# Projections by features: both token halves behind each other for every row group and product

## What is computed

```
xn  = layernorm(x)                                  # 625 x 1024
h   = relu(xn @ W_self0 + mean(xn) @ W_neigh0 + b0) # graph, first layer
x  += h @ W_self1 + mean(h) @ W_neigh1 + b1         # second layer
q, k, v = xn @ Wq, xn @ Wk, xn @ Wv                 # 16 heads of 64
q = softmax(q, features) / 8;  k = softmax(k, tokens)
x  += (q @ (k.T @ v)) @ Wo + bo
xn2 = layernorm(x)
gate, up = xn2 @ shared_gate_up                     # 1024 + 1024 columns
shared   = sigmoid(xn2 @ shared_gate_w) * ((silu(gate) * up) @ shared_down)
x  += routed(xn2, top 2 of 8 experts) + shared
```

## Time and profile before

| | before |
|---|---|
| median of 3 runs | 1042.11 us |
| the profiled execution | 1042.34 us |
| its span, first to last instruction | 1040.6 us |
| instructions | 16076 |
| matmuls, weight loads | 6128, 6128 |
| granted TensorE clock | 1.00 |
| HBM | 149 GB/s over the span |

### The profile page before, as it was taken

One profiled execution on the slowest core, in us unless ns is written; L12 is line 12 of the kernel. 1 busy time (PEld: TensorE's weight loads), 2 busy tenths in 40 slices (PEclk: granted clock), 3 DMA queues, 4 the chain that ended last, 5 costly groups with the idle time before them and its releaser, 6 DMA issues.

```text
span 1040.6 us, 16076 instructions
## 1 busy us (share of the span) xinstructions
PE 1024.7 (98%) x6128; PEld 905.3 (87%) x6128; DVE 650.5 (63%) x962; ACT 460.3 (44%) x731; POOL 77.2 (7%) x123
## 2 busy tenths in 40 slices
PE   7999999999999999999999999999999999999998
PEld 5889998787888899987878899998989789998977
DVE  6789968666655765334337364224878588776646
ACT  4423344557777523220122342212666576655530
POOL 6000010000000000000000017000100101000003
PEclk9999999999999999999999999999999999999999
DMA  9821212033212221262200524233789698887618
GB/s 351 314 82 52 71 41 82 11 110 123 81 63 79 82 81 43 106 213 82 81 1 1 181 82 122 89 116 125 265 300 342 223 339 311 278 283 245 227 38 299
DMA packets 76694, 156.44 MB, mean 150 GB/s; under 512 B 8489, under 2 KB 8987, under 8 KB 76618
## 3 DMA queue, kind: packets, MB, share of 16 engines
q1 hardware_dynamic: 65656, 127.30, 35.3%
q0 software_dynamic: 6416, 20.00, 5.5%
q10 hardware_dynamic: 4546, 8.10, 2.1%
HBM read 133.89 MB, written 21.49 MB: 149 GB/s over the span
## 4 chain that ended last, share of the span: by engine, by line
PE 87%; DVE 4%; ACT 3%; DMA 2%; DVEq 2%; issue 1%; POOL 1%; POOLq 0%; ACTq 0%; SPq 0%
PE ps L1988 20%; PE ps L1990 20%; PE ps L1989 20%; PE ps L2452 7%; PE ps L2477 3%; PE ps L2453 3%; PE ps L2087 1%; PE ps L2478 1%; PE ps L2319 1%; PE ps L2250 1%; PE ps L2320 1%; PE ps L2251 1%; PE ps L2101 1%; PE ps L2034 1%; DMA y_second<-expert_rows,slots 1%
## 5 line engine op out<-in xcount | busy, mean ns | idle before, releaser
L1199 DVE TENSOR_TENSOR w_lo<-w_raw,w_hi 128x2048 fp32r<-128x2048 f32 x41 | 93.1, 2289 | 38.6 <-ACT w_hi L801 36.5
L2452 PE MATMUL ps<-xe,w_hi 128*128 128x304 f32 (+2 forms) x384 | 107.1, 356 | 0.0
L1988 PE MATMUL ps<-w_hi,xt_hi 128*128 128x512 f32 (+1 forms) x240 | 95.9, 400 | 3.5 <-DVEq L1509 2.0
L801 ACT CAST w_hi<-w_raw 128x2048 fp32r<-128x2048 f32 x41 | 77.2, 1908 | 45.0 <-PE ps L2320 36.2
L1193 DVE TENSOR_TENSOR w_lo<-w_raw,w_hi 128x1024 fp32r<-128x1024 f32 x68 | 79.8, 1221 | 24.1 <-ACT w_hi L797 22.2
L2453 PE MATMUL ps<-xe,w_lo 128*128 128x152 f32 (+2 forms) x384 | 94.4, 246 | 0.0
L1990 PE MATMUL ps<-w_hi,xt_lo 128*128 128x512 f32 (+1 forms) x240 | 93.7, 390 | 0.0
L1989 PE MATMUL ps<-w_lo,xt_hi 128*128 128x512 f32 (+1 forms) x240 | 93.6, 390 | 0.0
L1193 DVE TENSOR_TENSOR w_lo<-w_late,w_hi 128x1024 fp32r<-128x1024 f32 x64 | 75.2, 1222 | 20.7 <-ACT w_hi L797 18.3
L797 ACT CAST w_hi<-w_late 128x1024 fp32r<-128x1024 f32 x64 | 63.0, 1054 | 38.7 <-PE ps L1990 18.4
L1988 PE MATMUL ps<-xt_hi,w_hi 128*128 128x314 f32 x256 | 79.4, 310 | 0.0
(11 more groups left out here) (371 smaller groups left out, 2365.4 us busy)
## 6 DMA issues: line engine op xcount, KB each, us to landing
w_raw<-in_L_ffn_w SPq DMA_DIRECT2D x64, 512.0 KB, 6.6
w_late<-in_L_ffn_w SPq DMA_DIRECT2D x64, 512.0 KB, 5.0
w_raw<-in_L_gnn_W_neigh SPq DMA_DIRECT2D x8, 1024.0 KB, 5.3
w_raw<-in_L_gnn_W_self SPq DMA_DIRECT2D x8, 1024.0 KB, 5.0
w_raw<-in_L_ffn_shared_gate_up SPq DMA_DIRECT2D x8, 1024.0 KB, 5.8
expert_rows<-ctx_s POOLq DMA_DIRECT2D x15, 512.0 KB, 13.5
w_raw<-in_L_mix_Wv SPq DMA_DIRECT2D x4, 1024.0 KB, 13.3
w_raw<-in_L_mix_Wk SPq DMA_DIRECT2D x4, 1024.0 KB, 5.0
```

Source lines behind the costliest of these rows:

```text
L801: copy(w_hi[b][:, s * HK:(s + 1) * HK, :], w_raw[s][:, :, :]).then_inc(hi_done, 1)
L1199: V_.tensor_tensor(w_lo[b][:, k, :], w_raw[s][:, :, :], as32(w_hi[b][:, k, :]), ALU.subtract).then_inc(lo_done, 1)
L1988: mat(out_ap, lh, rh, start=start, stop=False)
L2452: mat(PS(key)[:, a, 0:2 * width], wh[:, k, w_cols], xe[:, :, k, 0:width], start=k == 0, stop=False)
```

## The change

`by_features` no longer calls `passes` for all row groups of half 0 and then all of half 1. For each row group it goes through the three products, and for each product it issues the matmul of half 0 and the matmul of half 1. The first matmul of each half clears its bank (`start`), the last one closes it (`stop`). Callers and waits stay as they are; with `banks=(c,)` one half is left and the order is the old one.

```diff
             def by_features(key, n, operand, job, stop=True, banks=(0, 1)):
 
                 wh, wl = w_hi[job % 2], w_lo[job % 2]
-                for c in banks:
-                    for k in range(KF):
-                        w_cols = slice(n % HK * 128, (n % HK + 1) * 128)
-                        last = passes(PS(key)[:, c, 0:TH], (wh[:, k, w_cols], wl[:, k, w_cols]),
-                                      [t[:, k, c * TH:(c + 1) * TH] for t in operand], k == 0, stop and k == KF - 1)
+                w_cols = slice(n % HK * 128, (n % HK + 1) * 128)
+                for k in range(KF):
+                    for w, t in ((wh, operand[0]), (wh, operand[1]), (wl, operand[0])):
+                        for c in banks:
+                            last = mat(PS(key)[:, c, 0:TH], w[:, k, w_cols], t[:, k, c * TH:(c + 1) * TH],
+                                       start=k == 0 and w is wh and t is operand[0],
+                                       stop=stop and k == KF - 1 and w is wl)
                 return last
```

## The result

Over seven runs each, the kernel before takes 1041.82 us in the median (1041.46 to 1043.08), the changed one 1045.32 us (1044.65 to 1045.80). The ratio is 1.0030, with a 95% interval of 1.0020 to 1.0039: slower by 2.1 to 4.1 us. The profiled execution took 1044.65 us, with a span of 1042.9 us, against 1042.34 and 1040.6 before.

The account below looks back on a forecast made before the run. TensorE, busy 1024.7 of 1040.6 us, was taken to bound the kernel, through the distance between matmul starts. Three terms of 0 us each left the runs' median: forecast 1042.1 us, range 1039.6 to 1044.8 us.

Parts of the forecast that it names:

- all three stretches: Stretches holding the projections by features: PE always busy, so the end moves by the distance between matmul starts times their number.
- Term 1: Matmuls and weight loads of the projections by features: none removed or added, 0 us.
- Term 2 (a): PSUM bank switched after every matmul, 1380 more switches in 30 units: taken as 0, bounded at -7 to +7 us.
- a bank switch costs: Slower rival, 8%: output bank changes at every matmul in the 30 units; 5.4 ns x 1380 = 7.5 us, 1049.6 us.
- bound of 7 us: Limit on 1380 more bank switches, -7 to +7 us, from knowing a switch only to some 5 ns.
- Term 2 (b): More equal weights beside each other in the units, 480 more equal neighbours: 0 us.
- rival of cheaper equal weights: Faster rival, 7%: fixed part gone wherever the same weights follow, 480 x 15.1 ns = 7.2 us, 1034.9 us.
- Term 2 (c): Two halves of one operand read in turn in the units: mean stays 144.6 ns, bounded at -0.6 or +0.6 us.
- 15.1 ns of the 144.6 are fixed: Start distance of a 314-column matmul: 129.5 ns for columns, 15.1 ns fixed; only this could be won by another order.
- the rival built on it: Second faster rival, 4%: alternating banks frees an accumulation stall, at most the fixed part at 1380 switches, 20.8 us, 1021.3 us.
- Term 3: Waits and what follows a unit: nothing waits inside, readers start when they did, no DMA or queue moved, 0 us.

Follow-up runs that it names:

- e1: Kernel before, old order of operands and weights, but output to bank 0 and 1 in turn at every matmul: 6.94 us a unit.
- e2: Changed kernel, new order of operands, but the first 24 matmuls go to bank 0 and the other 24 to bank 1: 7.04 us a unit.
- e9: Changed kernel, but both matmuls of a product read half 0's slice, so one starting column instead of two: 6.94 us a unit.
- e10: Changed kernel with products ordered high x high, low weights, low tokens: 7.04 us a unit; 1044.61 us in one run.
- e3: Kernel before, for each row group three products of half 0, then of half 1: units of 7.04 or 6.94 us; 1043.29 us beside 1043.36 in one run.
- e5: Changed kernel, but half 1 reads from column 304 instead of 314: gate unit 7.12 us (148.3 ns a matmul), key 145.0 ns.
- e6: Changed kernel, but half 1 reads from column 312 instead of 314: gate unit 6.96 us (145.0 ns a matmul), key 143.3 ns.

## Why the prediction was wrong

- *PE sets the end in all three stretches, so the time moves by the distance of starts:* right. PE has no idle time there after the change either, and 2.84 us of longer units turned into a span 2.3 us longer. The 0.24 us made up behind the fourth key show that "by nothing else" holds only nearly: the kernel before had a short pause there that the view of waits doesn't list.
- *Term 1, no load or matmul is saved:* right, 6128 and 6128.
- *Term 2 (a), a bank switch costs 0:* right, shown by e1 and e2. The rival "a bank switch costs" named the right side by luck (its 5.4 ns a switch and 7.5 us stand against 2.1 ns a matmul and 3.5 us measured), and its mechanism is refuted. The bound of 7 us rested on 5 ns for a distance, while two times rounded to 0.01 us give one only to some 10 ns.
- *Term 2 (b), equal weights cost or give 0:* right in what the change pays. With the weights' pattern kept and the two starts taken away, e9 has the old pace; with the pattern changed and the starts kept, e10 has the new one. The rival of cheaper equal weights found no support.
- *Term 2 (c), the halves' slices in turn, "the same addresses are read equally often, so the mean should stay 144.6", bounded at 0.6 us:* this step failed. It took the distance to be a property of one matmul, and the 0.8 ns between the halves' means to be all that the start of a slice can do. It depends on the sequence of starts. Taking turns between columns 0 and 314 gives 146.7 ns, 2.1 ns above the mean of the two kept apart, which is outside either half's own pace (144.2 and 145.0 ns; unrounded, 144.5 and 144.7, so two thirds of the 0.8 ns were the view's rounding). 2.1 x 1440 = 3.0 us; the units have become 2.84 us longer in the trace, and 2.49 us of that are left behind the last up.
- *"15.1 ns of the 144.6 are fixed":* wrong as put. The distance depends on the sequence of slice starts; with 314 columns it was 143.3 to 148.3 ns in these runs. The page of the Trainium skill that I cited has 133.3 ns, as an estimate for a matmul by itself; no sequence came near it, and the rival built on it found nothing.
- *Term 3, nothing waits or is late:* right.
- *Range:* it ended at 1044.8 us, 0.5 below the median. What made it too narrow is that bound of 0.6 us on (c). No row of the kernel before showed two slices of one row read in turn, so (c) had no like in the rows, and the argument of equal addresses stood in for one. Had the range kept the whole 7 us of (a), it would have held the result, but by luck.

## What to carry to other kernels

Where TensorE is busy throughout, read its pace as start to start over a whole unit: durations of single matmuls (307 to 312 ns in both kernels) overlap and hide a loss of 1.4%. Interleaving two accumulations was free as regards banks and gained nothing from equal weights (6128 loads before and after); what cost was the changed sequence of start addresses of the moving operand. An order's price can't be had from the mean of its parts kept apart: try it, and vary the slice's start with it.

## What the runs showed of the hardware that I had not expected

At the granted clock of 1.00 the mean distances between starts of matmuls with a moving operand of 32 bits and 314 or 312 columns were 143.3, 144.3 to 144.6, 145.0, 145.4, 146.7 and 148.3 ns. Of these, 143.3, 145.0, 146.7 and 148.3 are 43, 43.5, 44 and 44.5 times 3.33 ns, which is 8 clocks at 2.4 GHz; the 226.3 ns of the earlier trace rows are 68 of them within the view's rounding. This reads as starts that fall into steps and lock into a pattern, also because one and the same order had two paces in one run (e3: 144.3 and 146.7 ns; e5: 145.0 and 148.3; e6: 143.3 and 145.0). In e3 and e5 it changed only behind other work, which suggests that the pattern is picked where a row of units starts. That is an explanation argued from the numbers; what makes the steps, how an address picks its pattern, and what picks between two patterns of one order was not shown and stays open.
